# Flamingo gated cross-attention with a mixture of experts: the first group's queries by direct copies from SBUF to SBUF, with other transfers reordered behind them

## The chip, the cores and the metric

The kernel runs on one core of one Trainium2 chip. The metric is the device time of one execution in microseconds (us). The engines are PE (matmuls; PEld is its weight load), DVE (vector), ACT (scalar activations), POOL (GpSimd) and SP (issues transfers). SP, ACT and POOL each issue transfers in the order of their program.

## What is computed

The input is 32 sequences of 128 tokens of width 128, with a context of 77 rows for each. A gated cross-attention with 16 heads of 8 columns is added to x, and then a gated mixture of experts.

```python
def _L0_xattn_ref(q, k, v, w_q, w_k, w_v, w_o):
    query, key_, value = proj(q, w_q), proj(k, w_k), proj(v, w_v)
    scores = einsum('bhqd,bhkd->bhqk', query, key_) / sqrt(8)
    x = einsum('bhqk,bhkd->bhqd', softmax(scores), value)
    return x.reshape(B, S, 128) @ w_o.T
...
x = x + tanh(g_xattn[0]) * _L0_xattn_ref(_layernorm(x), ctx_1024, ctx_1024, w_q, w_k, w_v, w_o)
x = x + tanh(g_ffn[0]) * _L0_ffn_ref(_layernorm(x), ...)   # shared expert + top 3 of 15 experts + x
```

## The kernel before

**Groups.** The attention works through 8 groups of 4 sequences (GB = 4); t counts the 32 sequences, g the groups. A group has a front part: statistics of x (`stats1_of`, `var1_of` on DVE), the reciprocal root (`pow1` on POOL), `shift1_of` on DVE, `apply1` on ACT (the normalised x), `front_x` on PE (transposes) and `xT_leaves` on ACT, and then `front_q` on PE (the query projection, 512 columns).

**Splitting.** The projection is kept as two parts: `lead_q` (ACT) writes the high part into `q_parts[:, 0]`, and `trail_q` (DVE) writes the rest into `q_parts[:, 1]`. Keys are split in the same way by `lead_k` and `trail_k`.

**Head layout.** `q_stack` holds three blocks of 32 partitions (r = 0 and 2 high part, r = 1 low part) for each of 4 head groups hg, and `k_heads` holds the keys of each head at their rows. PE cannot move rows between partitions by itself here, so the parts go out to DRAM (`q_split`, `k_split`) and come back rearranged: `send_q` and `load_q`, `send_k` and `load_k` on SP. `load_k` is 12 transfers for a group. In group 0 the work is cut up: the high and the low part of sequences 0 and 1 go out by ACT and SP (L743, L451), sequences 2 and 3 by POOL (L579), and `first_q` (L369) and L746 bring them back. POOL also zeroes the buffers of the second group in its own order (L581 to L587), and runs `pow1(2)` behind them.

**Attention.** For each t, `scores(t, hg)` on PE (L1332) gives scores for the row maxima, `maxima` on DVE (L911) takes them, `turn_max` (L1342) turns them and `max_rows` (ACT, L703) writes them into `q_stack`; `scores_t` (L1352) then gives the transposed scores less the maximum, `exps` (ACT, L711) the exponentials, `values(t)` (L1369) the weighted values. PE runs `scores(t + 1, ..)` in between `scores_t(t, ..)`. All engines execute in program order, tied together by semaphores. The prologue on PE is `front_k(0)`, `front_k(1)`, `front_x(0)`, `front_q(0)`, `front_v(0)`, `front_x(1)`, `scores(0, 0)`, `scores(0, 1)`, `front_q(1)`, `scores(0, 2)`, `scores(0, 3)`; then comes the loop over t.

**Afterwards.** Experts are chosen from the second layer norm; POOL scatters rows by expert during the attention, 76 blocks of 256 rows go through two layers, and POOL gathers them back.

## Time and profile before

| | us |
|---|---|
| median of 3 runs | 418.25 (416.89 to 419.85) |
| the profiled execution | 417.4 |
| its span | 415.6 |
| PE busy | 376.5 (91%) |
| DVE busy | 301.0 (72%) |
| ACT busy | 274.0 (66%) |
| POOL busy | 253.1 (61%) |

A busy share is a mean over the whole span. The change touches only the first 40 us or so, and there the reading goes by the order in time: when each engine reached an instruction, how long it had sat idle before, and what released it. A row of the timeline gives the start of a merged piece, its length, the engine, the line, and what was written from what.

### The profile page before, as it was taken

How to read it: one execution, taken by the hardware profiler on the slowest of the kernel's cores; microseconds unless marked ns; L12 is line 12 of the kernel's file. 1: busy time of each engine (PE TensorE's matmuls, PEld its weight loads, DVE VectorE, ACT ScalarE, POOL GpSimd, SP SyncE). 2: the span in 40 equal slices, each digit the busy share in tenths (PEclk: the TensorE clock that was granted, in tenths of full speed). 3: DMA queues.
4: the chain of work that ended last, by engine and by line, in shares of the span. 5: the costliest groups of instructions: out<-in, count | busy, mean ns of one | idle time of the engine just before them, and what ended most of it. 6: DMA issues, size and time to landing. Idle time of an engine off the chain costs nothing.

```text
span 415.6 us, 12422 instructions
## 1 busy us (share of the span) xinstructions
PE 376.5 (91%) x3840; PEld 334.3 (80%) x3840; DVE 301.0 (72%) x982; ACT 274.0 (66%) x609; POOL 253.1 (61%) x250
## 2 busy tenths in 40 slices
PE   3589999999999999999899988999999999999940
PEld 1267878787878788878899987899999997999940
DVE  6356877888888889786668976778777762687863
ACT  4338889988889897878666654566666666353500
POOL 6860120176767666675988977307777774777771
PEclk9999999999999999999999999999999999999985
DMA  4659573648363649634355447756666642233322
GB/s 146 180 148 244 175 210 111 165 136 235 118 202 122 190 131 306 225 104 153 123 179 157 155 149 232 231 179 187 193 197 203 200 142 69 77 79 102 82 76 69
DMA packets 57159, 66.30 MB, mean 160 GB/s; under 512 B 9092, under 2 KB 47748, under 8 KB 57096
## 3 DMA queue, kind: packets, MB, share of 16 engines
q1 hardware_dynamic: 49656, 51.49, 41.2%
q0 software_dynamic: 6352, 13.02, 10.8%
q10 hardware_dynamic: 1088, 1.00, 0.8%
q8 instruction: 33, 0.54, 0.5%
q14 instruction: 30, 0.25, 0.2%
HBM read 35.82 MB, written 29.29 MB: 157 GB/s over the span
## 4 chain that ended last, share of the span: by engine, by line
PE 58%; POOL 13%; DVE 8%; issue 7%; DMA 6%; ACT 4%; SPq 2%; POOLq 0%; ACTq 0%; DVEq 0%
PE psum L1493 13%; PE psum L1352 8%; POOL k_heads L625 8%; PE psum L1369 6%; PE psum L1473 4%; PE psum L1474 3%; PE psum L1332 3%; PE psum L1475 3%; PE psum L1463 3%; DVE max_cols L911 3%; POOL q_stack L625 2%; PE psum L1299 2%; PE psum L1342 2%; DMA w_raw<-rows_by_expert 2%; PE psum L1309 2%
## 5 line engine op out<-in xcount | busy, mean ns | idle before, releaser
L563 POOL DMA_INDIRECT rows_by_expert<-xn_all,row_of x96 | 96.1, 1001 | 44.6 <-ACT probs L711 22.5
L803 ACT ACTIVATE probs<-psum,b1c 128x256 f32<-128x256 f32 x152 | 63.8, 471 | 27.5 <-PE psum L1475 26.8
L1493 PE MATMUL psum<-w_all,probs 128*128 x608 | 80.1, 275 | 0.0
L1493 PEld LDWEIGHTS psum<-w_all,probs 128*128 128x128 f32 x608 | 74.2, 191 | 0.2
L625 POOL DMA_INDIRECT k_heads<-outs_by_block,back_row x60 | 57.9, 965 | 23.8 <-issue 16.4
L711 ACT ACTIVATE probs<-psum 77x512 f32<-77x512 f32 x128 | 68.9, 590 | 2.8 <-PE psum L1352 1.5
L911 DVE TENSOR_REDUCE max_cols<-psum 128x4 fp32r<-128x312 f32 x128 | 55.1, 472 | 7.0 <-PE psum L1332 6.5
L1352 PE MATMUL psum<-q_stack,k_heads 128*77 128x128 f32 x512 | 54.3, 243 | 0.8 <-ACT q_stack L703 0.5
L1352 PEld LDWEIGHTS psum<-q_stack,k_heads 128*77 128x77 f32 x512 | 43.8, 151 | 13.0 <-issue 5.6
L1053 DVE CAST w_ring<-w 128x512 fp32r x76 | 34.5, 454 | 22.1 <-issue 21.1
L1473 PE MATMUL psum<-q_parts,w_ring 128*128 128x256 f32 x152 | 49.1, 323 | 1.1 <-DVE q_parts L1041 1.1
L792 ACT ACTIVATE q_parts<-psum 128x256 fp32r<-128x256 f32 x76 | 29.1, 384 | 25.0 <-PE psum L1463 23.1
L1475 PE MATMUL psum<-q_parts,w_ring 128*128 128x256 f32 x152 | 42.7, 281 | 0.0
L1474 PE MATMUL psum<-q_parts,w_ring 128*128 128x256 f32 x152 | 42.7, 281 | 0.0
L1332 PE MATMUL psum<-k_heads,q_stack 128*128 128x312 f32 x128 | 39.1, 385 | 3.7 <-DMA q_stack<-q_split 3.5
L1041 DVE TENSOR_TENSOR q_parts<-psum,q_parts 128x256 fp32r<-128x256 f32 x76 | 31.8, 420 | 11.1 <-ACT q_parts L792 8.7
L1061 DVE TENSOR_TENSOR probs<-psum,probs 128x256 f32<-128x256 f32 x76 | 32.0, 421 | 8.1 <-PE psum L1493 4.0
L625 POOL DMA_INDIRECT v_pad<-outs_by_block,back_row x24 | 23.5, 980 | 22.1 <-DMA outs_by_block<-probs 15.1
L1369 PE MATMUL psum<-probs,v_pad 128*32 128x128 f32 x1024 | 34.6, 276 | 0.4 <-DVE placed L980 0.2
L1463 PE MATMUL psum<-ident_sb,w_raw 128*128 128x128 f32 x152 | 29.7, 278 | 4.5 <-DMA w_raw<-rows_by_expert 3.7
L1369 PEld LDWEIGHTS psum<-probs,v_pad 128*32 128x32 f32 x1024 | 26.0, 109 | 6.8 <-issue 3.1
L1609 PEld LDWEIGHTS psum<-w_shared,probs 128*128 128x128 f32 x256 | 29.7, 192 | 0.6
(155 smaller groups left out, 769.5 us busy)
## 6 DMA issues: line engine op xcount, KB each, us to landing
w_raw<-rows_by_expert SPq DMA_DIRECT2D x76, 128.0 KB
outs_by_block<-probs SPq DMA_DIRECT2D x76, 128.0 KB
q_stack<-q_split SPq DMA_DIRECT2D x21, 256.0 KB
q_split<-q_parts SPq DMA_DIRECT2D x7, 512.0 KB, 3.1
k_heads<-k_split SPq DMA_DIRECT2D x90, 39.0 KB
rows_by_expert<-zeros SPq DMA_DIRECT2D x27, 128.0 KB, 3.8
k_split<-w_all SPq DMA_DIRECT2D x8, 312.0 KB, 2.2
x_all<-in_x SPq DMA_DIRECT2D x8, 256.0 KB, 4.9
```

Source lines behind the costliest of these rows:

```text
L563: nc.gpsimd.indirect_dma_start(xd[:, :], bass.IndirectOffsetOnAxis(ap=row_of[:, r, m:m + 1], axis=0), xn2_all[:, r * GB + m // K, :], None ...
L625: nc.gpsimd.indirect_dma_start(back[j][:, k * GB + b, :], None, yd[half][:, :], bass.IndirectOffsetOnAxis(ap=back_row[:, j, b * K + k:b * ...
L711: nc.scalar.activation(probs[0:KV, n % 2, hg * 512:(hg + 1) * 512], st_ps[hg % 2][0:KV, :], ACT.Exp, scale=SCALE).then_inc(exp_done, 1)
L803: nc.scalar.activation(hid[u % 2][:, c, :], psum[:, 2 + c, 0:BLK], ACT.Gelu, bias=b1c[:, bass.ds(e * CR + (CS + c), 1)]).then_inc(gelu_don ...
L911: nc.vector.tensor_reduce(max_cols[:, n % 2, hg * HQ:(hg + 1) * HQ], s_ps[hg % 2][:, 0:HQ * KP].rearrange("q (h k) -> q h k", h=HQ), AX.X, ...
L1332: nc.tensor.matmul(s_ps[hg % 2][:, 0:HQ * KP].rearrange("q (h k) -> q h k", h=HQ), q_stack[:, g % 2, hg, b * S:(b + 1) * S], k_heads[:, g ...
L1352: ins = nc.tensor.matmul(st_ps[hg % 2][0:KV, hh * S:(hh + 1) * S], k_heads[:, g % 2, hg, hh, b, 0:KV], q_stack[:, g % 2, hg, b * S:(b + 1) ...
L1369: ins = nc.tensor.matmul(a_ps[c * 32:(c + 1) * 32, half * S:(half + 1) * S], v_pad[:, g % 2, at:at + 32], probs[:, n % 2, h * S:(h + 1) * ...
L1473: nc.tensor.matmul(ps, w1_now[u % NX][:, 0, c, :], xs_hi[u % 2], start=True, stop=False)
L1474: nc.tensor.matmul(ps, w1_now[u % NX][:, 0, c, :], xs_lo[u % 2], start=False, stop=False)
L1475: nc.tensor.matmul(ps, w1_now[u % NX][:, 1, c, :], xs_hi[u % 2], start=False, stop=True).then_inc(l1_done, 1)
L1493: ins = nc.tensor.matmul(psum[:, 4 + u % 2 * 2, b * P:(b + 1) * P], hid[u % 2][:, c, b * P:(b + 1) * P], w2_all[:, bass.ds(expert_of[u] * ...
```

## The change

The diff, cut to its core:

```diff
-            def first_q(b, r):
+            def direct_q(hg, r):
                 m = r % 2
-                sp.dma_start(q_stack[r * GR:(r + 1) * GR, 0, :, b * 2 * S:(b + 1) * 2 * S].bitcast(F32),
-                             qd[0].rearrange("(g p) m t -> m p g t", g=HG)[m, :, :, b * 2 * S:(b + 1) * 2 * S]).then_inc(q0_in[b], 16)
+                sp.dma_start(q_stack[r * GR:(r + 1) * GR, 0, hg, 0:S].bitcast(F32), q_parts[hg * GR:(hg + 1) * GR, m, 0:S].bitcast(F32)).then_inc(q00_in[hg], 16)
+
+            def first_q(part, cols):
+                sp.wait_ge(q0_sent[part], 16)
+                for r, m in enumerate((0, 1, 0)):
+                    sp.dma_start(q_stack[r * GR:(r + 1) * GR, 0, :, cols].bitcast(F32), qd[0].rearrange("(g p) m t -> m p g t", g=HG)[m, :, :, cols]
+                                 ).then_inc(q0_in[part], 16)
...
             load_picks(0)
-            load_k(0, 0, 6)
+            load_k(0, 0, 4)
+            sp.wait_ge(q_hi_ready, 1)
+            direct_q(1, 2)
+            direct_q(2, 0)
+            direct_q(2, 2)
+            direct_q(3, 0)
+            direct_q(3, 2)
+            sp.wait_ge(q_lo_ready, 1)
+            direct_q(3, 1)
+            first_q(0, slice(S, 2 * S))
             load_x(2)
-            sp.wait_ge(q_lo_ready, 1)
-            sp.dma_start(qd[0][:, 1, 0:2 * S], q_parts[:, 1, 0:2 * S].bitcast(F32)).then_inc(q0_lo_sent, 16)
-            sp.wait_ge(q0_hi_sent, 16)
-            first_q(0, 0)
-            sp.wait_ge(q0_lo_sent, 16)
-            first_q(0, 1)
             send_k(1)
-            sp.wait_ge(q0_rest_sent, 16)
-            for r in range(3):
-                first_q(1, r)
+            first_q(1, slice(2 * S, 4 * S))
             sp.wait_ge(k_zeroed, 2)
             load_picks(1)
-            load_k(1, 0, 3 * HQ)
+            load_k(1, 0, 2 * HQ)
             send_q(1)
+            load_k(1, 2 * HQ, 3 * HQ)
             load_ctx(2)
             load_q(1)
             load_x(3)
...
             pool.wait_ge(q_lo_ready, 1)
-            pool.dma_start(qd[0][:, :, 2 * S:4 * S], q_parts[:, :, 2 * S:4 * S].bitcast(F32)).then_inc(q0_rest_sent, 16)
+            for hg in range(3):
+                pool.dma_start(q_stack[GR:2 * GR, 0, hg, 0:S].bitcast(F32), q_parts[hg * GR:(hg + 1) * GR, 1, 0:S].bitcast(F32)).then_inc(q00_lo_in[hg], 16)
+            pool.dma_start(qd[0][:, :, S:2 * S], q_parts[:, :, S:2 * S].bitcast(F32)).then_inc(q0_sent[0], 16)
             pool.wait_ge(ln1_rstd, 2)
             pool.memset(probs[P // 2:P, 0], 0.0).then_inc(probs_zeroed[0], 1)
             pool.wait_ge(probs_zeroed[0], 1)
+            pool.dma_start(qd[0][:, :, 2 * S:4 * S], q_parts[:, :, 2 * S:4 * S].bitcast(F32)).then_inc(q0_sent[1], 16)
...
-            for hh in range(2, HQ):
-                act.dma_start(k_heads[GR + hh * DK:GR + (hh + 1) * DK, 0, :, hh].bitcast(F32).rearrange("p g b k -> p g (b k)"),
-                              kd[0].rearrange("(g h p) m c -> m h p g c", g=HG, h=HQ)[0, hh]).then_inc(k_in[0], 16)
+            load_k0(0)
+            load_k0(1)
             xT_leaves(0)
+            load_k0(2)
+            load_k0(3)
             lead_q(0)
+            lead_k(1)
             act.wait_ge(q_hi_ready, 1)
-            act.dma_start(qd[0][:, 0, 0:2 * S], q_parts[:, 0, 0:2 * S].bitcast(F32)).then_inc(q0_hi_sent, 16)
+            direct_q(0, 0)
+            direct_q(0, 2)
+            direct_q(1, 0)
             apply1(1, 0, GB)
...
-            lead_q(1)
...
+                if t == 0:
+                    lead_q(1)
                 exps(t, 2)
...
             trail_q(0)
+            trail_k(1)
             shift1_of(1)
             v_leaves(0)
-            trail_k(1)
...
-            trail_q(1)
             stats1_of(2)
...
                 if t == 0:
+                    trail_q(1)
                     dve.wait_ge(tanh_done, 1)
...
-                if n in (0, 2) and hg == 0:
-                    pe.wait_ge(q0_in[n // 2], 3 * 16)
+                if n == 0:
+                    pe.wait_ge(q00_in[hg], (2 if hg < 3 else 3) * 16)
+                    if hg < 3:
+                        pe.wait_ge(q00_lo_in[hg], 16)
+                elif n in (1, 2) and hg == 0:
+                    pe.wait_ge(q0_in[n - 1], 3 * 16)
...
-            front_x(1)
             scores(0, 0)
             scores(0, 1)
-            front_q(1)
+            front_x(1)
             scores(0, 2)
             scores(0, 3)
...
+                if t == 0:
+                    front_q(1)
```

Sequence 0's queries now go from `q_parts` straight to `q_stack` in 12 copies of 32 partitions by 128 elements: 3 on ACT, 6 on SP, 3 on POOL. Sequence 1 goes through DRAM alone (`first_q(0, ..)`), sequences 2 and 3 as before but sent after a memset of POOL. `load_x(2)` and `send_k(1)` stand behind sequence 1 on SP. The new `load_k0(hh)` on ACT is the transfer that stood in the loop there.

On PE, from the first scores on, before (`psum<-w_all 128x512` is `front_q(1)`, `psum<-ident_sb,w_all` is `front_x(1)`):

```order
L1292 MATMUL psum<-ident_sb,w_all 128x128 [waits xT_out,xn_ready]
L1292 MATMUL psum<-ident_sb,w_all 128x128 x3
L1332 MATMUL psum<-k_heads,q_stack 128x312 [waits k0_in,k0_rest_in,k_lo_ready,q0_0_in,q_zeroed,picks0_in]
L1332 MATMUL psum<-k_heads,q_stack 128x312
L1299 MATMUL psum<-w_all 128x512 [waits q_lo_ready,xT_out]
L1332 MATMUL psum<-k_heads,q_stack 128x312 [waits max_done] x2
L1342 MATMUL psum<-ident_r,max_cols 4x128 [waits v_out,max_done,id_ready]
L1342 MATMUL psum<-ident_r,max_cols 4x128 x3
L1332 MATMUL psum<-k_heads,q_stack 128x312 [waits max_done] x2
L1352 MATMUL psum<-q_stack,k_heads 77x128 [waits m_ready]
L1352 MATMUL psum<-q_stack,k_heads 77x128 x7
```

and on PE in the changed kernel:

```order
L1359 MATMUL psum<-k_heads,q_stack 128x312 [waits k0_rest_in,k0_in,q00_0_in,k_lo_ready,q00_0_lo_in,q_zeroed,picks0_in]
L1359 MATMUL psum<-k_heads,q_stack 128x312 [waits q00_1_lo_in,q00_1_in]
L1315 MATMUL psum<-ident_sb,w_all 128x128 [waits xT_out,xn_ready]
L1315 MATMUL psum<-ident_sb,w_all 128x128 x3
L1359 MATMUL psum<-k_heads,q_stack 128x312 [waits max_done,q00_2_lo_in,q00_2_in]
L1359 MATMUL psum<-k_heads,q_stack 128x312 [waits max_done,q00_3_in]
L1369 MATMUL psum<-ident_r,max_cols 4x128 [waits v_out,max_done,id_ready]
L1369 MATMUL psum<-ident_r,max_cols 4x128 x3
L1359 MATMUL psum<-k_heads,q_stack 128x312 [waits max_done,q0_next_in]
L1359 MATMUL psum<-k_heads,q_stack 128x312 [waits max_done]
L1379 MATMUL psum<-q_stack,k_heads 77x128 [waits m_ready]
L1379 MATMUL psum<-q_stack,k_heads 77x128 x7
```

`front_x(1)` moved behind the first two scores, `front_q(1)` is gone from here (it stands behind the last row), and sequence 1's scores wait for `q0_next_in`.

On POOL, between `pow1(1)` and `pow1(2)`, before:

```order
L579 DMA q_split<-q_parts 256x1x256 [waits q_lo_ready]
L581 MEMSET probs 64x2048 [waits ln1_rstd]
L583 MEMSET k_heads 128x4992 [waits probs0_zeroed]
L585 MEMSET q_stack 32x2048 [waits k_zeroed]
L587 MEMSET probs 64x2048 [waits q_zeroed]
L546 TENSOR_SCALAR var<-mv 128x4 [waits xn_ready,ln1_step,probs1_zeroed]
```

and in the changed kernel:

```order
L589 DMA q_stack<-q_parts 32x128 [waits q_lo_ready]
L589 DMA q_stack<-q_parts 32x128 x2
L590 DMA q_split<-q_parts 256x1x128
L592 MEMSET probs 64x2048 [waits ln1_rstd]
L594 DMA q_split<-q_parts 256x1x256 [waits probs0_zeroed]
L595 MEMSET k_heads 128x4992
L597 MEMSET q_stack 32x2048 [waits k_zeroed]
L599 MEMSET probs 64x2048 [waits q_zeroed]
L555 TENSOR_SCALAR var<-mv 128x4 [waits xn_ready,ln1_step,probs1_zeroed]
```

Four more transfers stand ahead of the last memset, and behind it is still `pow1(2)`.

On ACT, around the first exponentials, in the changed kernel:

```order
L718 ACTIVATE q_stack<-psum 4x4x128 [waits mT_done]
L726 ACTIVATE probs<-psum 77x512 [waits probs0_zeroed,st_done]
L726 ACTIVATE probs<-psum 77x512 [waits st_done]
L698 ACTIVATE w_all<-x_all,shift,rstd 128x128 [waits xT_done,shift1_ready]
L698 ACTIVATE w_all<-x_all,shift,rstd 128x128
L691 ACTIVATE q_parts<-psum 128x512 [waits q00_2_in,q00_2_lo_in,q00_1_lo_in,q00_3_in,q00_1_in,q0_next_sent,q00_0_lo_in,q0_rest_sent,q00_0_in,q_done]
L726 ACTIVATE probs<-psum 77x512 [waits st_done] x2
L718 ACTIVATE q_stack<-psum 4x4x128 [waits mT_done]
```

The row L691 is `lead_q(1)`; it stood ahead of the first row before, and is now between `apply1(2, 0, 2)` and the last two exponentials of sequence 0.

## Rows read from the trace of the kernel before

**Rows 1.** The chain that ended last, to 32 us: start, length, what

```profile
15.05 3.51 DMA q_split<-q_parts
18.58 2.77 DMA q_stack<-q_split
...
22.35 1.71 PE psum L1299 x2
```

**Rows 2.** Timeline of PE: start, length, idle before and its releaser

```profile
16.83 1.12 PE L1292 MATMUL psum<-ident_sb,w_all 128*128 128x128 f32 x4 [1.53 <-ACT w_all L683]
21.49 0.86 PE L1332 MATMUL psum<-k_heads,q_stack 128*128 128x312 f32 x2 [3.54 <-DMA q_stack<-q_split]
...
25.71 0.83 PE L1332 MATMUL psum<-k_heads,q_stack 128*128 128x312 f32 x2
...
30.63 0.48 PE L1342 MATMUL psum<-ident_r,max_cols 128*4 128x128 f32 x4
...
31.39 1.08 PE L1369 MATMUL psum<-probs,v_pad 128*32 128x128 f32 x32
...
34.98 1.07 PE L1299 MATMUL psum<-w_all 128*128 128x512 f32 x2
...
40.25 0.69 PE L1332 MATMUL psum<-k_heads,q_stack 128*128 128x312 f32 x2
```

**Rows 3.** Timeline of ACT

```profile
13.63 0.60 ACT L676 ACTIVATE q_parts<-psum 128x512 fp32r<-128x512 f32 x1 [2.23 <-PE psum L1299]
...
28.76 0.88 ACT L683 ACTIVATE w_all<-x_all,shift,rstd 128x128 f32<-128x128 f32 x2 [0.25 <-DVE shift L884]
29.55 1.06 ACT L711 ACTIVATE probs<-psum 77x512 f32<-77x512 f32 x2
31.15 0.59 ACT L703 ACTIVATE q_stack<-psum 4x512 fp32r<-4x512 f32 x1 [0.55 <-PE psum L1342]
```

**Rows 4.** Timeline of DVE

```profile
26.93 0.84 DVE L911 TENSOR_REDUCE max_cols<-psum 128x4 fp32r<-128x312 f32 x2
28.56 0.16 DVE L884 SCALAR_TENSOR_TENSOR shift<-mv,rstd 128x4 f32<-128x4 f32 x1 [0.79 <-POOL rstd L548]
```

**Rows 5.** Timeline of POOL

```profile
15.32 0.74 POOL L579 DMA_DIRECT2D q_split<-q_parts  x1 [1.28 <-DVE q_parts L892]
...
24.14 1.80 POOL L587 MEMSET probs<- 64x2048 f32 x1
27.18 0.23 POOL L546 TENSOR_SCALAR var<-mv 128x4 f32<-128x4 f32 x1 [1.23 <-issue]
```

**Rows 6.** Tile k_heads to 40 us: durations of an issue, ns min/median/max

```profile
L575 POOL DMA_DIRECT2D k_heads<-k_split x4: 544/565/850, 10.1 to 12.1; - x4
```

**Rows 7.** Line L369: the same for SP, and landing from issue

```profile
L369 SPq DMA_DIRECT2D q_stack<-q_split x5: 313/430/464, 17.7 to 20.5; - x5
...
DMA to landing us min/median/max: 2.5/3.4/3.5
```

**Rows 8.** Transfers of the first 60 us: size each, median us to landing

```profile
x_all<-in_x SPq DMA_DIRECT2D x6, 256.0 KB, 4.3
...
q_split<-q_parts POOLq DMA_DIRECT2D x1, 256.0 KB, 3.8
...
k_heads<-k_split POOLq DMA_DIRECT2D x4, 39.0 KB, 3.1
```

**Rows 9.** Timeline of SP (SPq: an issue)

```profile
22.99 6.26 SPq L351 DMA_DIRECT2D k_heads<-k_split  x12
...
32.40 1.94 SPq L379 DMA_DIRECT2D q_stack<-q_split  x3
```

**Rows 10.** Windows: busy (instructions) of PE, PEld, DVE, ACT, POOL, granted clock, DMA share, GB/s

```profile
20.00:25.00 5.00, 3.09 (x6) 1.70 (x6) 2.95 (x7) 0.60 (x1) 4.88 (x3) 1.00 0.63 187
...
40.00:100.00 60.00, 58.55 (x794) 47.83 (x793) 48.38 (x187) 52.94 (x119) 16.20 (x21) 1.00 0.62 172
```

24 lines of the change are left out of this document (15 added, 9 removed).

## The prediction, made before the changed kernel ran

> **What bounds the kernel now.** I read three views in this order. First the windows and the page: between 40 and 100 us PE is busy 58.55 of 60 us [rows 10]. Whatever time PE loses or wins before 40 us is therefore passed on almost whole, and I look for the shift of PE's work at about that point. Second the chain that ended last: before the first scores it is not an engine at all but two transfers in a row, 3.51 us out to DRAM and 2.77 us back [rows 1]. The reader should see in PE's timeline that the first scores start at 21.49 after 3.54 us of idleness [rows 2]. Third the timelines of ACT, DVE and POOL between 25 and 32 us, because a gain at 21 us is only worth what the next slow link lets through. That link runs POOL, DVE, ACT: POOL ends its last memset at 25.94 and starts `pow1(2)` at 27.18 [rows 5], DVE has sat idle 0.79 us for it when it does the shift at 28.56 [rows 4], and ACT's `apply1(2, 0, 2)` starts at 28.76, straight behind it; only then come the last two exponentials of sequence 0, 29.55 to 30.61, and the next maxima at 31.15 [rows 3]. PE takes the values of sequence 0 at 31.39 [rows 2], 0.78 us after those exponentials ended.
>
> **The first scores: 3.1 us earlier.** The high part is ready at 14.23 (13.63 and 0.60) [rows 3], the low part at 15.04, where the chain's transfer starts [rows 1]. A copy of 32 x 128 elements from SBUF to SBUF occurs nowhere in the trace. On the hardware queues its landing is bounded by 2.5 and 3.5 us [rows 7]; on POOL's by 2.5 below and by the 3.1 us of its key transfers above [rows 8]; being the smallest, I take 2.5 on SP and ACT and 2.9 on POOL. POOL issues the low part of head group 0 at 15.32 [rows 5], so it lands at 18.2. ACT issues its three behind `lead_k(1)` and DVE trails both splits by then, so POOL is last. SP's six issues at 0.31 to 0.46 us [rows 7] end near 16.5. First scores: 18.3 to 18.4, 3.1 us ahead of 21.49. `front_x(1)`, 1.12 us [rows 2], now lies behind two of them, in time in which DVE works anyway. The last maxima of sequence 0 and their turning shift by the same 3 us.
>
> **Sequence 1: 1.6 us of it are left.** Its queries still take the two transfers. POOL has three copies first, at 0.57 us (0.54 to 0.85) an issue [rows 6]: 15.32 + 1.7 = 17.0. Landing of 128 KB from POOL: 3.1 to 3.8 [rows 8], I take 3.4, so 20.4. SP then issues three reads, the last at 21.2, and it lands 2.8 later (2.5 to 3.5) [rows 7]: `scores(1, 0)` at about 24.1 against 25.71 [rows 2].
>
> From there PE had no long pause up to `turn_max(1)` at 30.63 [rows 2], that is 4.9 us of work. `front_q(1)` is now in it, at 1.71 us [rows 1]. 24.1 + 4.9 + 1.7 = 30.7: PE has given back the gain and stands as before.
>
> **x of the third group.** `load_x(2)` stood at 14.2 and is now behind those reads, at 21.7. With 4.3 us to landing [rows 8] it arrives at 26.0, where DVE once waited for nothing. Its statistics take 1.2 us, so the maxima of sequence 1 start at 27.2 against 26.93 [rows 4]. This cover has no slack left: each us later from here is later for DVE.
>
> **POOL: 1.1 us later, and ACT with it.** Four issues more: three copies at 0.57 and one send of at most 0.74 [rows 5, 6], 2.3 us (bounds 1.7 and 3.3). POOL works without a pause from 15.32 to 25.94 [rows 5], so its last memset now ends at 28.25. `pow1(2)` can start there, 27.18 before: 1.1 us late. Behind it in order: the shift on DVE (28.56 becomes 29.65), behind that the last two maxima of sequence 1; on ACT `apply1(2, 0, 2)`, 28.76 becomes 29.85. Then stands `lead_q(1)`, 0.60 us [rows 3], in the old time a piece that lay in an idle wait. The two exponentials end at 30.61 + 1.1 + 0.6 = 32.3. PE wants them at 31.4 to 31.5: it loses 0.8 to 0.9 us there. Maxima of sequence 1 on ACT go from 31.15 [rows 3] to 32.3, 1.15 us late, and PE's later parts wait for them no longer than that.
>
> **What is late next.** `q_lo_ready` of the second group comes at about 32.0, where SP used to send it right behind its 12 key loads at 29.30 [rows 9]. SP sends eight loads ahead now and waits; it sends at 32.0, and with the 3.1 to 3.8 us of such sends [rows 8] the three reads go out from 35.3 to 37.2 instead of 32.40 to 34.34 [rows 9]. They are wanted at 40.25 [rows 2] plus the 0.9, and the last, issued near 36.2, has 5 us for 3.5 to 4.5 us of landing. `load_x(3)` goes out at 37.2, wanted by DVE at 41.5, 4.3 us on: no slack. I cost both at nothing and keep 1 us for the range. The weights and constants behind them are first used in the iteration t = 3, so I take them as covered.
>
> **The pace of PE.** The projection of 512 columns takes 1.71 us at 22.35 in the chain [rows 1] and its pair of instructions spans 1.07 us at 34.98 [rows 2]: PE works at half pace early on, although the granted clock reads 1.00 in the window 20 to 25 [rows 10], the higher of the two levels. The weight of `front_q(1)` in the sum above is that of the early pace. The Trainium skill (TensorE: Matmul & The Clock Gate, "HAM oscillation — how this bites in real kernels") says that the clock is low after idle time and rises with sustained activity. This trace agrees in the durations, not in the column. By that page PE, which now works on from 24.1 without the old pause, would come to the full pace earlier, and the moved projection would cost about 0.9 us, the 1.07 less the overlap. PE would then reach the values of sequence 0 at 30.6, and would wait longer for ACT: the sum by the page is the same as by the rows.
>
> **The sum.** 417.4 us of the profiled execution (span 415.6 and 1.8 around it) + 0.9 = 418.3. The profiled execution lies 0.85 below the median of the runs, 418.25. Against that median the same shift gives 419.1.
>
> **The rivals.**
>
> *Faster: the start's gain gets through.* If POOL issues the small copies quicker than its key transfers, under 0.2 us each, the shift on DVE comes at 28.4. Then exponentials end at 31.0 and PE sets the pace, earlier by the part of the half-pace work that it now does sooner, 0.5 to 1.3 us. The time would be 416.9 to 417.8 against the median, 417.3. It decides where POOL's last memset ends: before 27.1 us it is this case. For it speaks only that such small copies are unmeasured; against it, 0.54 is the least of four issues.
>
> *Late queries or x of the next groups.* SP is a single file: if the two reads of sequence 1 land at their upper bound and the x behind them too, DVE starts the maxima of sequence 1 at 28.2 instead of 27.2, and `load_x(3)` or the second group's reads come 1 us late on top. 0.9 + 1 + 1 = 2.9 us: 421.1. It decides from x in later than 26.9.
>
> *PE's half pace lasts longer.* The pauses before `scores(1, 0)` and before the values of sequence 0 could put off the full pace from about 30.5 to about 34 us. Work of that stretch, 3.5 us, would take twice as long: 422.5 with the 0.9. Against it speaks that PE works without a gap from 24.1 to 31.5, longer than the stretch from 25.71 to 30.63 that went before the turn [rows 2].
>
> *The change doesn't shorten the start*: the copies take as long as the two transfers, the first scores at 21 us. Then all of the delays stand as well, 1.5 to 3 us: 420.5.
>
> **How the numbers follow.** Chances: forecast 0.50, gain gets through 0.22, late queries or x 0.17, half pace longer 0.06, no shorter start 0.05. The time is the likeliest's, 419.1. The range takes the faster rival to 417.0 below and the late transfers to 421.8 above; outside it remain the lower tail and the longest delays, and the scatter of a median of runs that spread over 3 us. One per cent, 4.2 us, is about what a measurement of this kernel tells from no change. Faster by that would need more than the 3.1 us the start can give: 0.02. Slower by that needs the half pace or several late transfers: 0.06. Within it: 0.92.
>
> **What the new profile would show.** First scores at 18.3 (right if within 0.5 us), `scores(1, 0)` near 24.1 behind 1 to 1.5 us of idle PE on a transfer. POOL's last memset before `pow1(2)` ends at 28.2, the shift of the third group is done at 29.7, and ACT's second pair of exponentials ends near 32.3, with PE idle or stretched ahead of the values of sequence 0. If PE is at those values before 31.4, the forecast is wrong and the faster rival holds. If POOL has finished but DVE sits on x, it is the third case. From 40 us on every piece should stand about 0.9 us later; if the distance changes behind that, something that I don't name here is at work.

## The result and the profile after

The changed kernel takes 421.16 us (median of 20 runs, 419.65 to 423.44), the kernel before 418.23 us (20 runs beside them, 416.58 to 420.37). The ratio is 1.0065, 95% interval 1.0047 to 1.0083: 2.9 us slower. The profiled execution took 421.27 us with a span of 419.5, against 417.4 and 415.6 before; its granted clock was 0.98 in both.

PE of the kernel after in its timeline (start, length, idle before it and its releaser), to be held against [rows 2]:

```profile
20.79 0.97 PE L1359 MATMUL psum<-k_heads,q_stack 128*128 128x312 f32 x2 [5.27 <-DMA q_stack<-q_parts]
...
24.78 0.89 PE L1359 MATMUL psum<-k_heads,q_stack 128*128 128x312 f32 x2 [0.30 <-DMA q_stack<-q_split]
...
32.78 1.08 PE L1396 MATMUL psum<-probs,v_pad 128*32 128x128 f32 x32 [0.83 <-ACT probs L726]
...
43.41 0.53 PE L1359 MATMUL psum<-k_heads,q_stack 128*128 128x312 f32 x2 [1.36 <-issue]
```

First scores come at 20.79 instead of 21.49, sequence 1's at 24.78 instead of 25.71. At the values of sequence 0 PE is 1.39 us behind (32.78 against 31.39) and has waited 0.83 us for ACT. At the first scores of the second group, `scores(4, 0)`, it is 3.16 us behind (43.41 against 40.25), after 1.36 us of a new idle wait. The gain at the start is lost again by 33 us, as forecast; but the loss goes on past 40 us. The row at 43.41 names no releaser. `scores(4, 0)` waits for the three reads of the second group's queries, and in the trace the last arrival on their semaphore is at 43.21, 0.20 us ahead of PE's start.

The loss comes in steps. For a ruler I use the start of `max_rows` on ACT in a few sequences t, as the distance to the kernel before (which has it at 25.95, 31.15, 45.32, 65.31 and 185.91 us for t = 0, 1, 4, 8, 31), and the start of the last expert block's result on DVE (344.33 us before). One profiled execution of each kernel stands behind a row:

```
us later than before   t=0    t=1    t=4    t=8    t=31   last block
after                 -1.44  +1.61  +2.99  +5.84  +5.81   +3.89
```

There is a step of 1.6 at t = 1, one of 1.4 up to t = 4 and one of 2.9 up to t = 8. Then the distance is constant, and the expert blocks between 255 and 282 us take 1.9 back. From t = 31 to the last block the number changes by -1.9 to +0.6 from kernel to kernel. Much of it goes with PE's waits for transfers of rows to the experts: with the wait for ACT at the same line they sum to 4.2 us before and 2.9 us after, and over all kernels run here to between 2.9 and 5.0 us, lowest where the last number falls most. Why these waits differ isn't shown, so below I argue from the columns up to t = 31 only.

**The step at t = 1.** POOL, DVE and ACT of the kernel after in their timelines (the rows that answer to [rows 3 to 5]):

```profile
15.54 1.60 POOL L589 DMA_DIRECT2D q_stack<-q_parts  x3 [1.33 <-DVE q_parts L915]
17.12 0.75 POOL L590 DMA_DIRECT2D q_split<-q_parts  x1
...
26.93 1.80 POOL L599 MEMSET probs<- 64x2048 f32 x1
28.82 0.23 POOL L555 TENSOR_SCALAR var<-mv 128x4 f32<-128x4 f32 x1
```

```profile
26.20 0.87 DVE L894 BATCH_NORM_STATS2 stats<-x_all 128x6 f32<-128x128 f32 x4 [2.41 <-DMA x_all<-in_x]
...
27.40 0.84 DVE L934 TENSOR_REDUCE max_cols<-psum 128x4 fp32r<-128x312 f32 x2
30.21 0.17 DVE L907 SCALAR_TENSOR_TENSOR shift<-mv,rstd 128x4 f32<-128x4 f32 x1 [1.97 <-POOL rstd L557]
```

```profile
30.41 0.88 ACT L698 ACTIVATE w_all<-x_all,shift,rstd 128x128 f32<-128x128 f32 x2 [3.11 <-DVE shift L907]
31.20 0.58 ACT L691 ACTIVATE q_parts<-psum 128x512 fp32r<-128x512 f32 x1
31.68 1.06 ACT L726 ACTIVATE probs<-psum 77x512 f32<-77x512 f32 x2
32.76 0.59 ACT L718 ACTIVATE q_stack<-psum 4x512 fp32r<-4x512 f32 x1
```

POOL ends its last memset at 28.73 and starts `pow1(2)` right behind, at 28.82 instead of 27.18. DVE, done with its maxima, sits 1.97 us idle for it. ACT sits 3.11 us, does `apply1(2, 0, 2)`, then the new `lead_q(1)`, and only then the exponentials, 31.68 instead of 29.55. PE's 0.83 us of idleness end 0.04 us behind them.

**The steps at t = 4 and t = 8.** SP's timeline after (SPq is an issue; L363 sends the queries of a group out, L386 reads them back, L345 and L353 the same for keys):

```profile
27.14 4.66 SPq L353 DMA_DIRECT2D k_heads<-k_split  x8
32.53 0.35 SPq L363 DMA_DIRECT2D q_split<-q_parts  x1
32.92 1.51 SPq L353 DMA_DIRECT2D k_heads<-k_split  x4
...
37.28 1.27 SPq L386 DMA_DIRECT2D q_stack<-q_split  x3
...
46.37 1.36 SPq L345 DMA_DIRECT2D k_split<-w_all  x1
52.09 4.74 SPq L353 DMA_DIRECT2D k_heads<-k_split  x12
...
57.64 1.47 SPq L386 DMA_DIRECT2D q_stack<-q_split  x3
```

and of SP before, the same steps behind those of [rows 9]:

```profile
29.30 0.35 SPq L361 DMA_DIRECT2D q_split<-q_parts  x1
...
43.02 0.33 SPq L343 DMA_DIRECT2D k_split<-w_all  x1
47.50 4.50 SPq L351 DMA_DIRECT2D k_heads<-k_split  x12
...
52.77 1.47 SPq L379 DMA_DIRECT2D q_stack<-q_split  x3
```

The send of the second group's queries is 3.2 us later (32.53 against 29.30), its reads 4.9 us (37.28 against 32.40), because the send itself needed 4.7 us to land, against 3.1 before. `scores(4, 0)` starts 6.1 us behind the first of those reads. The send of the third group's keys is 3.4 us late and their first read 4.6 us; the reads of the third group's queries stand behind 12 of them and go out 4.9 us late (57.64 against 52.77). Two transfers carry this in the list of transfers (size, us to landing), in the stretches 32.4 to 32.7 and 46 to 52:

```profile
q_split<-q_parts SPq DMA_DIRECT2D x1, 512.0 KB, 4.7
```

```profile
k_split<-w_all SPq DMA_DIRECT2D x1, 312.0 KB, 5.6
```

What holds the third group's keys up is a row of DVE. The queries' reads being late, `load_x(3)`, x of the fourth group, goes out behind them in SP's file and late too (38.59 against 34.38). DVE sits idle for that x; only then come its maxima of sequence 4 and the split of the keys:

```profile
43.84 0.87 DVE L894 BATCH_NORM_STATS2 stats<-x_all 128x6 f32<-128x128 f32 x4 [1.81 <-DMA x_all<-in_x]
...
45.80 0.47 DVE L911 TENSOR_TENSOR w_all<-psum,w_all 128x312 fp32r<-128x312 f32 x1
```

The split ends at 46.27 and the send goes out at 46.37; before, these were 42.96 and 43.02. SP had come through its own file at 46.18, so DVE and SP were ready almost together. The landing of this send, 5.6 us against 4.4 before, adds 1.2 us to the 3.4.

In the chain that ended last the second stall is a row of its own, and PE's timeline shows it:

```profile
58.68 5.96 DMA q_stack<-q_split
64.69 0.89 PE psum L1359 x2
```

```profile
62.07 0.74 PE L1306 MATMUL psum<-w_all 128*128 128x312 f32 x2
64.69 0.89 PE L1359 MATMUL psum<-k_heads,q_stack 128*128 128x312 f32 x2 [1.88 <-DMA q_stack<-q_split]
...
65.72 1.94 PE L1396 MATMUL psum<-probs,v_pad 128*32 128x128 f32 x32
...
71.23 1.08 PE L1396 MATMUL psum<-probs,v_pad 128*32 128x128 f32 x32
```

PE waits 1.88 us, and the values behind that wait take 1.94 us where the same 32 matmuls take 1.08 later. The windows of the kernel after say why (columns as in [rows 10]: the granted clock is the third number from the end):

```profile
60.00:64.00 4.00, 2.81 (x25) 1.97 (x23) 3.22 (x16) 3.56 (x8) 0.00 (x0) 1.00 1.06 239
64.00:66.00 2.00, 1.31 (x11) 0.92 (x15) 0.61 (x3) 0.83 (x3) 1.26 (x2) 0.66 1.01 361
66.00:68.00 2.00, 2.00 (x35) 1.53 (x28) 0.78 (x2) 0.70 (x3) 0.00 (x0) 0.50 0.15 61
```

The granted clock falls to 0.50, the lower of the two levels (1.2 GHz), from about 64.6 to 68 us, after PE had stood still from 62.81 to 64.69. The Trainium skill (TensorE: Matmul & The Clock Gate, "HAM oscillation — how this bites in real kernels") says that a wait for a transfer can throttle the engine again, so that the next piece starts slowly; here the trace agrees that it can, in the clock and in 1.94 against 1.08 us. But the wait alone doesn't decide: keys_ahead below waits 1.92 us at the same place and keeps 1.00. The step at t = 8, 2.9 us, is thus 1.9 us of wait and about 0.9 us of slow values and scores.

### The profile page after: what moved, and what is told of

Same layout as the page of the kernel before. It is cut to its first block, busy times and chain, and to the rows that moved or that the text cites. A ratio compares the mean times of both kernels' runs of the same rounds, so it can differ in the third digit from the quotient of the medians.

```text
span 419.5 us, 12440 instructions
## 1 busy us (share of the span) xinstructions
PE 377.6 (90%) x3840; PEld 335.0 (80%) x3840; DVE 300.8 (72%) x982; ACT 273.9 (65%) x609; POOL 255.4 (61%) x254
## 4 chain that ended last, share of the span: by engine, by line
PE 54%; POOL 14%; DVE 8%; DMA 7%; issue 7%; SPq 5%; ACT 2%; POOLq 0%; DVEq 0%; ACTq 0%
PE psum L1519 13%; POOL k_heads L637 8%; PE psum L1379 7%; PE psum L1396 6%; PE psum L1499 4%; PE psum L1500 3%; PE psum L1501 3%; PE psum L1489 3%; PE psum L1359 3%; DVE max_cols L934 3%; POOL q_stack L637 2%; PE psum L1369 2%; PE psum L1322 2%; POOL expd L642 1%; DMA q_stack<-q_split 1%
## 5 line engine op out<-in xcount | busy, mean ns | idle before, releaser
L826 ACT ACTIVATE probs<-psum,b1c 128x256 f32<-128x256 f32 x152 | 63.8, 470 | 26.0 <-PE psum L1501 25.3
L1359 PEld LDWEIGHTS psum<-k_heads,q_stack 128*128 128x128 f32 x128 | 21.4, 200 | 15.2 <-issue 10.3
```

Of the source, the lines that this page charges most:

```text
L826: nc.scalar.activation(hid[u % 2][:, c, :], psum[:, 2 + c, 0:BLK], ACT.Gelu, bias=b1c[:, bass.ds(e * CR + (CS + c), 1)]).then_inc(gelu_don ...
L1359: nc.tensor.matmul(s_ps[hg % 2][:, 0:HQ * KP].rearrange("q (h k) -> q h k", h=HQ), q_stack[:, g % 2, hg, b * S:(b + 1) * S], k_heads[:, g ...
```

## The experiments

The expectations weigh two theories: 1, the lateness comes through POOL, DVE and ACT; 2, it comes through SP's single file of transfers. "After-based" or "before-based" says which kernel the edit starts from. The table has the staircase of each, from its profiled execution, and its ratio to the kernel before in runs beside it:

```
us later than before   t=0    t=1    t=4    t=8    t=31   last   ratio (95% interval)
after                 -1.44  +1.61  +2.99  +5.84  +5.81  +3.89  1.0065 (1.0047 to 1.0083)
pow_first             -1.48  +0.40  +1.22  +1.93  +1.95  +1.49  1.0036 (1.0002 to 1.0071)
q1_early              +0.50  +1.08  +1.10  +1.09  +1.07  +1.30  1.0006 (0.9969 to 1.0042)
q1_late_alone         -0.66  +0.62  +0.62  +0.60  +0.59  +1.09  1.0007 (0.9964 to 1.0049)
send_mid_alone        +0.05  -0.24  -0.24  +0.38  +0.31  -0.61  0.9961 (0.9932 to 0.9990)
send_mid_again        +0.54  +0.96  +1.12  +1.12  +1.10  +0.93  0.9997 (0.9979 to 1.0014)
late_weights          -2.57  +1.25  +2.44  +3.50  +3.52  +3.15  1.0045 (1.0028 to 1.0062)
mid_late              +0.49  -0.04  -0.25  -0.25  -0.23  +0.34  0.9988 (0.9971 to 1.0006)
all_three             +0.44  +0.17  +2.08  +2.98  +3.07  +1.85  1.0015 (0.9994 to 1.0037)
no_pool               -2.45  -0.49  +2.74  +2.55  +2.55  +2.84  0.9999 (0.9974 to 1.0024)
keys_ahead            -1.95  +1.19  +2.03  +3.30  +3.32  +3.25  1.0083 (1.0054 to 1.0112)
no_pool_ahead         -1.84  -0.31  +1.38  +1.55  +1.55  +0.22  1.0008 (0.9985 to 1.0030)
all_ahead             -2.86  -0.95  -1.16  -1.04  -1.05  -2.65  0.9967 (0.9949 to 0.9985)
```

send_mid_alone and send_mid_again are one and the same kernel. Their staircases differ by 1.2 to 1.4 us at t = 1 and 4 and by 0.8 from t = 8 on, their ratios by 0.0036. 0.5 of it stands at t = 0 already. The rest is TensorE's clock: its record in send_mid_alone begins with 1.00 at 29.8 us, the windows 28 to 30 and 30 to 32 us of send_mid_again read 0.73 and 0.50, and the same eight matmuls of `front_v(1)` that start there at 29.4 and 29.7 take 1.25 and 1.93 us. So 0.7 us at t = 1 can come from the clock alone. Differences of that size in one row alone carry nothing; the steps of the kernel after, 1.4 and 2.9 us, carry weight because PE's idle rows show them.

**pow_first** (after-based): the reciprocal root of the third group goes ahead of POOL's last memset.

```diff
             pool.wait_ge(q_zeroed, 2)
+            pow1(2)
+            pool.wait_ge(ln1_rstd, 3)
             pool.memset(probs[P // 2:P, 1], 0.0).then_inc(probs_zeroed[1], 1)
...
-                if t == 0:
-                    pow1(2)
```

> The changed kernel with the reciprocal root of the third group put ahead of POOL's last memset of the prologue (the last memset waits for it). Theory 1, POOL's zeroing order is the root: the shift on DVE comes at 28.9 instead of 30.2, the last two exponentials of sequence 0 end near 31.4, the first step of the staircase (1.6 us at sequence 1) shrinks to about 0.3, and the second and third step shrink too because the second group's queries are ready 1.3 us earlier: 2 to 4 us faster than the changed kernel, ratio to before 0.997 to 1.001. Theory 2, the single file of transfers on SP is the larger part: only the first step goes, SP's eight key loads still end at 31.8 and its later waits stay, the steps at sequences 4 and 8 stand: ratio to before 1.003 to 1.006.

POOL and ACT in the timelines of this kernel:

```profile
27.61 0.23 POOL L555 TENSOR_SCALAR var<-mv 128x4 f32<-128x4 f32 x1 [1.14 <-issue]
...
29.03 1.80 POOL L601 MEMSET probs<- 64x2048 f32 x1
```

```profile
29.20 0.88 ACT L698 ACTIVATE w_all<-x_all,shift,rstd 128x128 f32<-128x128 f32 x2 [2.03 <-DVE shift L907]
...
30.47 1.06 ACT L726 ACTIVATE probs<-psum 77x512 f32<-77x512 f32 x2
```

The root starts 1.21 us earlier than after, and the exponentials by the same 1.21. The step at t = 1 falls from 1.61 to 0.40. The chain POOL, DVE, ACT, PE is real; the clock has no part in it, since `max_rows` of sequence 1 follows the exponentials without a pause in both kernels (31.55 behind 31.53, 32.76 behind 32.74). It also takes 3.9 us off t = 31, much more than 1.2: SP sends the queries 0.97 us earlier, reads them 2.0 us earlier (35.28) and all behind with it. So both theories have a part, and the two later steps shrink without vanishing. The runs show less than the staircase: 1.0036, with an interval (1.0002 to 1.0071) that overlaps that of after.

**q1_early** (after-based): the query projection of sequences 1 to 3 and its two splits go back to their old place in each engine's order; the SBUF-to-SBUF copies and SP's new order stay.

```diff
             front_x(1)
+            front_q(1)
             scores(0, 2)
...
-                if t == 0:
-                    front_q(1)
```

> The changed kernel with the projection of the second group's queries and both its copies (front_q, lead_q, trail_q of group 1) back at the place that they had before. Theory 1 (lateness comes through ACT and POOL): the exponentials of sequence 0 are 0.6 us earlier, the queries are ready at 27 and sent at 31.9, 0.6 us earlier than 32.5: 0.6 to 1.2 us faster than the changed kernel, ratio 1.003 to 1.005. Theory 2 (SP's file): the send still waits for eight key loads and goes 0.6 us earlier, and the steps at sequences 4 and 8 stay within 0.6 us of what they were: ratio 1.005.

The start's gain is gone (t = 0 comes 0.5 late), t = 1 stands at 1.1, and behind it there is no step: +1.1 from t = 1 to 31. The send goes out at 30.81 and is read from 33.96. The 0.6 between t = 0 and t = 1 is no wait: PE works without a pause from 25.83 to the values at 32.50, but its clock reads 0.50 in the window 30 to 32 us and `front_v(1)` takes 1.93 us, where it took 1.55 before. That can be this execution's alone, as the pair of send_mid runs shows. Both theories had expected 1.003 to 1.005; the runs gave 1.0006, and the steps at t = 4 and 8 that theory 2 kept are gone.

**q1_late_alone** (before-based): the reverse, only the projection and its splits moved later.

> The kernel before with only the projection of the second group's queries and its two copies moved into sequence 0, as the change does. The queries are ready at about 30.9 instead of 25.8 and are sent 1.6 us later than 29.3. Theory 1: the slack of the second group's queries (wanted at 40.3) covers that, and PE loses at most the 0.6 us of the copy on ACT but wins 1.7 us of projection at the first scores: ratio 0.997 to 1.001. Theory 2: the 1.6 us pass through SP to the keys of the third group; a stall of 1 to 2 us appears at sequence 8: ratio 1.002 to 1.005.

+0.6 at t = 1 and never more: in the profiled execution, 418.51 us, the move by itself costs half a microsecond and brings neither of the later steps. But the ten runs of this kernel go from 416.47 to 421.35 with a median of 419.54, against 418.15 before, and the interval, 0.9964 to 1.0049, leaves a loss of half a per cent open. What the slower executions did wasn't profiled.

**send_mid_alone** and, once more, **send_mid_again** (before-based): only the send between the key loads.

```diff
-            load_k(1, 0, 3 * HQ)
+            load_k(1, 0, 2 * HQ)
             send_q(1)
+            load_k(1, 2 * HQ, 3 * HQ)
```

> The kernel before with only the next queries sent between key loads (eight loads, the send, four loads). They are ready at 25.8, so the send goes at 27.9 instead of 29.3 and its landing is hidden by the last four loads. Theory 1: no change, since no engine waits for these queries before: ratio 0.999 to 1.001. Theory 2: SP is free of its 2.3 us wait, and x, the weights and the keys of the third group go out 1.5 to 2.5 us sooner; the staircase has no step in the kernel before, so at most 0.5 us faster: ratio 0.998 to 1.000.

> The kernel before with only the next queries sent between key loads, once more with more rounds: the first measurement gave 0.9961 (0.9932 to 0.9990), its profile a PE that stood 0.4 us behind from sequence 8 on and no cause for a gain. Theory 2 expects 0.999 to 1.001 and that the first ratio was mostly scatter; if it is again 0.996, something outside the first 70 us gains.

0.9961 at first, 0.9997 the second time, with staircases of +0.3 and +1.1. The part by itself does nothing that these runs can tell. To read a gain from the first of them would have been to read scatter, although its interval leaves 1 out.

**late_weights** (after-based): eight transfers (six constants of the experts, two of zeros) leave SP's file between `load_x(3)` and `load_x(4)`, and go behind the keys' send of the third group; DVE waits for them four sequences later. **mid_late** is send_mid_alone with the same edit, **all_three** is after with pow_first, q1_early and this edit.

```diff
+                if t == 3:
+                    for dst, src in (...):
+                        sp.dma_start(dst, src).then_inc(moe_in, 16)
...
-                if t == 3:
+                if t == 7:
                     dve.wait_ge(moe_in, MOE_IN)
```

> The changed kernel with the six loads of expert constants and the two transfers of zeros moved on SP from behind the first two weight loads to behind the sending of the third group's keys (and their first use on DVE from t = 3 to t = 7). Theory 2 (SP's single file behind a burst of transfers): the third group's keys are sent about 4 us sooner and land in about 3.5 instead of 5.6 us, so the third step of the staircase, 2.9 us at sequence 8 with the low clock behind it, goes, while the second one at sequence 4, which lies ahead of the moved transfers, stays: 1.5 to 3 us faster than the changed kernel, ratio to before 0.999 to 1.003. Theory 1 (POOL and ACT alone): the keys' send waits for the late queries and PE, not for the burst, and nothing changes: ratio 1.0065.

> The kernel before with the next queries sent between key loads and with the expert constants and zeros moved behind the third group's keys. Theory 2: SP and the transfer engines are freed around 35 to 45 us, but in the kernel before no step stands in the staircase there, so at most the 0.6 us that appeared at sequence 8 with the first edit alone goes: ratio 0.994 to 0.997. Theory 1: as the first edit alone, 0.996.

> The changed kernel with all three repairs: root of the third group ahead of POOL's last memset, the second group's query projection at its old place, the expert constants behind the third group's keys. Both theories together: first step below zero or near it (0.4 and 1.1 us singly, and each took a different part), second and third step gone: PE at sequence 8 within 0.5 us of before, ratio 0.996 to 1.000. If a step remains, its cause is neither of the two.

mid_late shows that the moved transfers cost nothing by themselves (-0.2 us, 0.9988; 0.994 to 0.997 was expected). late_weights missed its expectation: 1.0045, not 0.999 to 1.003. The third group's keys were to be sent 4 us sooner, and were sent 0.55 us sooner (45.82), though SP had nothing to do from 39.8 us on: the send follows DVE's split of the keys, which ends at 45.75. They did land sooner, in 3.0 us instead of 5.6 (3.1 in all_three, 2.4 in mid_late), without the eight transfers ahead of them; but these now stand between the send and its reads, which go out at 51.08, 1.0 us sooner. So a late SP isn't what makes this send late; the late x and PE's own stall are enough. In late_weights the step between t = 4 and t = 8 falls from 2.9 to 1.1, yet PE still waits there, and the granted clock reads 1.00 in both windows from 64 to 68:

```profile
63.84 0.57 PE L1360 MATMUL psum<-k_heads,q_stack 128*128 128x312 f32 x2 [1.71 <-DMA q_stack<-q_split]
```

So the fall of the clock is not what every such wait brings: 1.71 us of idleness left it alone here, 1.88 us did not in the kernel after. all_three (1.0015, where 0.996 to 1.000 was expected) has hardly a step at t = 1 and still +1.9 up to t = 4: its send goes out at 31.02 and its reads at 35.80. What stands between the two is again a send that took 4.8 us to land. A step that remains was to have a cause outside the two theories; this landing is one.

**no_pool** (after-based): POOL's three copies of the low part move to SP, three of the high part change places between SP and ACT; POOL keeps its two sends, one more than before.

```diff
             pool.wait_ge(q_lo_ready, 1)
-            for hg in range(3):
-                pool.dma_start(q_stack[GR:2 * GR, 0, hg, 0:S].bitcast(F32), ...).then_inc(q00_lo_in[hg], 16)
...
+            direct_q(0, 2)
+            sp.wait_ge(q_lo_ready, 1)
+            direct_q(0, 1)
+            direct_q(1, 1)
```

> The changed kernel with all twelve direct copies on SP (8) and ACT (4), in the order of the head groups, and none on POOL. POOL's last memset ends 1.6 us sooner and the root of the third group with it. Theory 1: first step down from 1.6 to about 0.3 us, the later steps shrink with it (as when the root was put ahead of the memset: 1.1 and 0.9 us); ratio 1.001 to 1.004. Theory 2: the two more issues on SP, 0.6 us each, delay sequence 1's queries little, and its file stays late: ratio 1.005 to 1.008. On the copies: if a copy's landing is its own latency (3.4 us for the first on a queue), the first scores start at 18.8; if it is the crowd of small copies (5 us for later ones), at 20 to 21 as now.

PE of this kernel:

```profile
19.46 1.29 PE L1360 MATMUL psum<-k_heads,q_stack 128*128 128x312 f32 x2 [4.45 <-DMA q_stack<-q_parts]
...
30.69 1.08 PE L1397 MATMUL psum<-probs,v_pad 128*32 128x128 f32 x32 [0.35 <-ACT probs L726]
...
41.64 0.53 PE L1360 MATMUL psum<-k_heads,q_stack 128*128 128x312 f32 x2 [1.70 <-issue]
...
42.21 1.74 PE L1397 MATMUL psum<-probs,v_pad 128*32 128x128 f32 x32
```

and its window 44 to 46 us:

```profile
44.00:46.00 2.00, 2.00 (x13) 2.00 (x14) 0.77 (x3) 1.49 (x3) 0.82 (x1) 0.53 1.13 368
```

The first scores come 1.3 us earlier than after, between the two values that were expected (18.8 for a copy's own latency, 20 to 21 for the crowd), and at the values of sequence 0 PE is ahead of the kernel before by 0.70: without POOL's copies the root comes at 26.73 and t = 1 stands 0.49 us ahead. The wait at `scores(4, 0)` is there all the same, 1.70 us. The step between t = 3 and t = 4 is larger, 3.45 us (-0.71 to +2.74), because here the clock fell behind this wait: 0.62 in the window 42 to 44 us, 0.53 in the next, and the values take 1.74 us instead of 1.08. The profiled execution, 420.23 us, lies 2.2 us above this kernel's median of 418.04. A fall of the clock that comes in some executions and not in others would do that; one without it wasn't profiled, so this stays open.

**keys_ahead** (after-based): x of the third group and the second group's keys go ahead of the reads of sequence 1. **no_pool_ahead** is both edits together.

```diff
-            first_q(0, slice(S, 2 * S))
-            load_x(2)
             send_k(1)
+            load_x(2)
+            first_q(0, slice(S, 2 * S))
```

> The changed kernel with the sending of the second group's keys and the load of the third group's x put back on SP ahead of the wait for sequence 1's queries; nothing else. Theory 2, as it stands after the runs so far (a stall at a group's first scores wherever the first of its three query reads goes out less than 6 to 7 us before they are wanted): keys are sent at 18.4 instead of 23.6, but POOL clears their buffer only at 25.0, so the eight loads start at about 25.9 instead of 27.1; x arrives 3 us sooner. The reads of the second group's queries go out about 1 us sooner than 37.3, since the copy on ACT still comes at 31.2: the step at sequence 4 loses about 1 us, the first step stays at 1.3 to 1.6. Ratio 1.002 to 1.005. Theory 1 (POOL's order alone): DVE still waits for the root, no change: 1.0065.

> The last one and the copies off POOL together. POOL clears the key buffer 1.6 us sooner, the keys have been sent by then. Theory 2: both limits on the key loads are gone, they start at 24.2, the queries are sent at about 30.4 (bound by the copy on ACT) and land in 4 us, reads go out at 34.2: the step at sequence 4 falls from 3.2 to about 1.5 us, first step as without POOL's copies (0.5 us gained). Ratio 0.996 to 0.999. If sequence 4 still shows 3 us, it isn't the time of the query reads.

DVE of keys_ahead (timeline):

```profile
23.20 0.86 DVE L894 BATCH_NORM_STATS2 stats<-x_all 128x6 f32<-128x128 f32 x4
...
29.79 0.16 DVE L907 SCALAR_TENSOR_TENSOR shift<-mv,rstd 128x4 f32<-128x4 f32 x1 [4.13 <-POOL rstd L557]
```

x is there 3 us earlier, and DVE waits 4.13 us for POOL alone: the shift moves by 0.42 us, the step at t = 1 from 1.61 to 1.19. That speaks against the rival in which x decides the first step. PE waits 1.92 us at `scores(8, 0)`, until 63.64, and the clock stays at 1.00 behind it. The rest of this run stays open: its staircase is 2.5 us better than that of after at t = 31, its ratio, 1.0083, is not (1.002 to 1.005 was expected). no_pool_ahead has still 1.31 us of idleness at `scores(4, 0)` (41.43), and a ratio of 1.0008, where 0.996 to 0.999 was expected.

**all_ahead** (no_pool_ahead, and): `front_q(1)` directly behind `turn_max(0)` on PE, `lead_q(1)` directly behind the first `max_rows`, `trail_q(1)` ahead of the maxima of sequence 1.

```diff
             turn_max(0)
+            front_q(1)
             for t in range(B):
...
                 max_rows(t)
+                if t == 0:
+                    lead_q(1)
```

> The last one and the second group's query projection right behind the turning of sequence 0's maxima, its copy on ACT straight behind those maxima: the queries are ready at 26.8 instead of 30.4, so they are sent behind eight key loads at about 29.0 and the reads go out at 33. Theory 2: that is earlier than 34, as in the variant with the early projection, and no step is left at sequences 4 and 8; PE stands 0.5 to 1 us ahead of before from there on: ratio 0.995 to 0.998. If a step remains, the direct copies cost something that I haven't found.

PE of this kernel:

```profile
39.09 0.69 PE L1360 MATMUL psum<-k_heads,q_stack 128*128 128x312 f32 x2
...
59.28 0.57 PE L1360 MATMUL psum<-k_heads,q_stack 128*128 128x312 f32 x2 [0.63 <-DMA q_stack<-q_split]
```

SP's send is back at its old time (29.12, before 29.30), the reads too (32.61, before 32.40). PE doesn't wait at `scores(4, 0)` and is 1.16 us ahead there. The staircase stays at -1.0 to -1.2 from t = 1 to t = 31, and the ratio is 0.9967 (0.9949 to 0.9985), median 416.31 us (415.58 to 417.66). Against the kernel after the start's gain gets through. Against the kernel before the lead is of the size that send_mid_alone showed and its repetition didn't, and this kernel wasn't run again. The clock helped as well: it reads 1.00 from the window 26 to 28 us on, while the same work still ran slowly before (`front_v(1)` 1.04 against 1.55 us). PE's pieces from 25 to 30 us are 1.7 us shorter for it, and PE waited 1.3 us more in between, so an estimate of the clock's share in the lead is 0.4 us.

**The threshold in one table.** For the kernel before and ten others, by the time at which SP sends the second group's queries and first reads them; "last in" is the last arrival on the semaphore of the three reads:

```
kernel          send    first read   last in   scores(4,0)   PE idle ahead of it
before          29.30   32.40        38.21     40.25         none
all_ahead       29.12   32.61        38.68     39.09         none
q1_late_alone   30.84   33.70        39.62     40.87         none
q1_early        30.81   33.96        40.14     41.35         none
no_pool_ahead   30.61   33.90        41.23     41.43         1.31
no_pool         30.43   35.14        41.44     41.64         1.70
pow_first       31.56   35.28        41.22     41.42         0.59
keys_ahead      32.10   35.47        41.90     42.10         0.48
late_weights    32.17   35.49        42.32     42.52         0.83
all_three       31.02   35.80        42.28     42.48         1.67
after           32.53   37.28        43.21     43.41         1.36
```

In all seven stalled kernels PE starts 0.20 us behind the last arrival, in the four others the reads were in 0.4 to 2.0 us ahead of it: these reads are what `scores(4, 0)` waits for. Of the stalled ones PE starts 6.1 to 7.5 us behind the first read. With reads up to 33.7 nothing waits; from 35.1 on it waits each time. At 33.9 there is one of each: the reads of q1_early were in at 40.14, with PE there at 41.35; those of no_pool_ahead came in only at 41.23, with PE ready from 40.12. The landing of the send, 3.1 us before and 4.7 to 4.8 in after, no_pool and all_three, decides as much as the time of its issue. It is 3.3 us in late_weights, where the same four key loads follow the send, so those alone don't explain it.

## Why the prediction was right in one half and wrong in the other

**What bounds the kernel** held: from 33 us to t = 31 the distance changes only where PE is seen to wait or to slow down. That the total fell into the range is luck in part, as the account below says.

**First scores.** 18.3 was forecast, 20.79 measured. The term that failed is the landing of the copies. I took 2.5 us on SP and ACT and 2.9 on POOL. Landings by line of the kernel after, for L371 (SP), L750 (ACT) and L589 (POOL):

```profile
L371 SPq DMA_DIRECT2D q_stack<-q_parts x6: 586/591/621, 14.5 to 17.7; - x6
...
DMA to landing us min/median/max: 2.7/3.2/5.0
```

```profile
L750 ACTq DMA_DIRECT2D q_stack<-q_parts x3: 612/632/864, 14.5 to 16.0; - x3
...
DMA to landing us min/median/max: 3.4/5.1/5.4
```

```profile
L589 POOL DMA_DIRECT2D q_stack<-q_parts x3: 496/507/606, 15.5 to 16.6; - x3
...
DMA to landing us min/median/max: 4.6/4.8/4.8
```

A median of 5.1 on ACT and 4.8 on POOL, outside my bound of 3.5. "Being the smallest" was no reason: five of the six copies on ACT and POOL needed 4.6 us or more, above the far larger send of [rows 1] with its 3.51. Nor was POOL last: PE waited for the second copy of ACT, issued at 15.14 and in at 20.55; POOL's first was in at 20.36. And an issue on SP takes 0.59 us, not 0.31 to 0.46. So the gain is 0.7 us, not 3.1.

**Sequence 1.** 24.1 forecast, 24.78 measured: POOL's send starts at 17.12 (17.0 forecast) and needs 4.7 us, above my 3.1 to 3.8. Since this gain was to be given back by 31 us anyway, and PE still had 0.83 us to wait at the values, neither miss reached the end.

**x of the third group** landed at 26.18 (26.0), the maxima of sequence 1 started at 27.40 (27.2). Right.

**POOL and ACT.** Last memset ended at 28.73 (28.25 forecast), shift at 30.21 (29.65), exponentials ended at 32.74 (32.3), `max_rows` of sequence 1 1.6 us late (1.15). The mechanism was right, and pow_first, no_pool and keys_ahead show it; the size was 0.5 us short because POOL came to `pow1(2)` 0.48 us later than summed: it began at 15.54 instead of 15.32, and stood 0.30 us at 19.7 for the memset that its second send was put behind. The prediction's own terms, three issues at 0.57 and one at 0.74, sum to 2.45 us and not to 2.3. PE's wait, 0.83 us, is what I wrote, but it starts from 31.9 and not from 31.4, so 1.39 us were lost by then, not 0.8 to 0.9.

**"I cost both at nothing."** This is the step that failed. The reads of the second group were forecast from 35.3 and went out at 37.28, half a microsecond of it from a send at 32.53 instead of 32.0, the rest from that send's landing, 4.75 us instead of 3.3. PE came for them at 42.05 (43.41 less its idle 1.36), 0.9 us later than the 41.15 I had counted with, and still had to wait: the last read was issued near 38.1 and in at 43.21, 5.1 us, where I had 3.5 to 4.5 us for a landing. The second of the "both", `load_x(3)`, failed with it: it went out at 38.59 instead of 37.2 and needed 5.2 us instead of 4.3, and DVE stood 1.81 us for it. And I stopped one group too soon: through that x and PE's stall the third group's keys were split late, their send was slow itself (5.6 us), the queries' reads stand behind the keys' in SP's file, and all this cost PE another 2.9 us at 62 to 68 us with the fall of the clock. It was the rival "late queries" by its mechanism, but at a higher price (+5.8 at t = 31, where I had 2.9 for it) and from another start (the queries' send, and x of the fourth group behind it, not x of the third). The chance of 0.17 was too small: a cover that I had called "no slack" in the same paragraph should not have been priced at nothing.

**What would show it wrong** was said: from 40 us on each piece 0.9 us later, and if the distance changes, something I don't name is at work. It changed from 1.6 to 5.8. The total, 421.2 against 419.1, lies in the range only because that rival's price was in it, and because the expert phase gave 1.9 of the 5.8 back in the profiled execution. As far as the prediction goes that part is luck: 1.3 of the 1.9 us are shorter waits of PE at the experts' rows, which the prediction didn't treat and whose cause I don't know.

**The pace of PE.** The prediction found the early projection at half pace while the column of the granted clock read 1.00. The column was wrong, not the durations: the traces of before and after hold no record of the clock ahead of 30.34 and 30.51 us, and the view prints 1.00 there. Nine of the other kernels' traces do have one, and in all of them the clock is at 0.50, the level of 1.2 GHz, from 18 or 19 us on and rises between 25.3 and 32.1 us (in send_mid_again it falls once more, from 28.9 to 32.3). The same projection, `front_q(1)`, takes 1.91 us in send_mid_alone, without a record, and 1.91 us in send_mid_again, whose windows read 0.50 there. The rival "half pace lasts longer" (whose terms sum to 422.6, not 422.5) did not come in the kernel after: its record begins with 1.00, only 0.17 us later than that of before; it did in q1_early and send_mid_again, at about 0.4 to 0.7 us for `front_v(1)` alone (1.93 us against 1.55 before and 1.25 in send_mid_alone). What the new profile doesn't bear out is that the higher level comes earlier because PE works on through 24 to 31 us.

**The rival "gain gets through"** was right about where it decides (POOL's last memset) and wrong about how: not quicker issues of the copies on POOL, but none of them, and even then only with the projection put early enough for SP's send at 29.1 (all_ahead).

## What to carry to other kernels

When a step is moved on one engine, follow the file of transfers that stands behind it until it has caught up, for two or three groups and not for one: a queue in program order hands on its lateness, to the engines that wait for what stands further back in it as well (here x for DVE, and by DVE the next keys), and each late transfer can meet a burst that makes it slower. Price a small transfer by a measured landing of its own kind and on its own queue, issued in the same crowd; its size says little. If a gain at the start is to be kept, look for the first engine behind it that has new work to do (here POOL's three issues and ACT's split) and take the work away from there first.

## What I had not expected of the hardware

- Copies of 16 KB from SBUF to SBUF, twelve of them on three queues, issued from 14.5 to 17.7 us, landed 2.7 to 5.4 us after issue. The transfer engines weren't full in that time: this is the window 16 to 17 us of the kernel after, half of their time busy at 85 GB/s.

```profile
16.00:17.00 1.00, 0.00 (x0) 0.00 (x0) 0.62 (x2) 0.26 (x1) 1.00 (x3) 1.00 0.53 85
```

  Why they land late isn't settled. With POOL's three moved to SP, SP's eight have a median of 2.5 us (all_ahead), 2.9 us (no_pool) and 3.1 us (no_pool_ahead), against 3.2 us for its six in the kernel after.
- Between 43 and 49 us after, the DMA share is over 1 (1.13 at 329 GB/s in 46 to 47 us), and the 312 KB send of keys needs 5.6 us there; with eight transfers taken out ahead of it, it needs 3.0 us (late_weights) and 3.1 us (all_three).
- The length of PE's last idle wait doesn't tell whether the granted clock falls: it fell to 0.50 behind 1.88 us in the kernel after and behind 1.70 us in no_pool, and stayed at 1.00 behind 1.92 us in keys_ahead and 1.71 us in late_weights. In send_mid_again it fell near 29 us, with no wait of PE over 0.75 us since the first scores.
- A clock column can read 1.00 where the trace holds no record. Five traces of the fourteen have none ahead of about 30 us; the durations of a piece that stands in all of them tell the level.
- Two profiled executions of one and the same kernel can differ by 0.5 to 1.4 us in their staircase, and its ratio from 0.9961 to 0.9997, with an interval of 0.9932 to 0.9990 for the first, which leaves 1 out.
